# Gather and segment-sum of a graph layer on one core: one-hots in one operation, place and column loaded, slots released by marker products

## The reference

```python
h = jnp.maximum(_layernorm(x, axis=-1), 0.0)
xs = h[src]
for i in range(4):
    msgs = msgs + jnp.where((edge_types == i)[:, None], xs @ W[i] + b[i], 0.0)
return x + jax.ops.segment_sum(msgs, dst, num_segments=12500)
```

## Time and profile before

| | us |
|---|---|
| median of 3 runs | 2328.6 |
| lowest, highest | 2311.18, 2332.2 |
| profiled execution, its own time | 2344.42 |
| its span | 2342.7 |

### The profile page before, as it was taken

The page is one execution under the profiler, slowest core; times in us unless marked ns, Lnnn a source line. Parts: engine busy times, 40 slices in busy tenths (PEclk is TensorE's granted clock), DMA queues, the critical chain, the costliest instruction groups (busy, mean ns, idle before and its releaser), DMA issues.

```text
span 2342.7 us, 19295 instructions
## 1 busy us (share of the span) xinstructions
PE 873.5 (37%) x3921; PEld 641.9 (27%) x3922; DVE 705.6 (30%) x1734; ACT 134.7 (6%) x384; POOL 1484.2 (63%) x1573
## 2 busy tenths in 40 slices
PE   6774133233433343334343433343334233421233
PEld 2232122223322323222222232223222232321123
DVE  5554123233232323232323232323232233221123
ACT  3331000000000000000000000000000000000000
POOL 6666665756665666666666666666666666666763
PEclk8886566666665666666666665666666576665666
DMA  8663111111111111111111111111111111111231
GB/s 247 213 202 106 45 45 40 48 36 46 47 45 40 46 47 44 43 45 47 45 46 45 47 45 42 45 47 45 42 45 47 44 43 45 47 45 45 66 107 53
DMA packets 95454, 144.73 MB, mean 62 GB/s; under 512 B 27481, under 2 KB 57683, under 8 KB 95363
## 3 DMA queue, kind: packets, MB, share of 16 engines
q0 software_dynamic: 50016, 102.50, 16.8%
q1 hardware_dynamic: 40567, 38.92, 5.0%
q10 hardware_dynamic: 4780, 2.51, 0.4%
HBM read 111.73 MB, written 32.09 MB: 61 GB/s over the span
## 4 chain that ended last, share of the span: by engine, by line
another core or an unknown queue 29%; issue 25%; DVEq 24%; PE 10%; DVE 10%; ACT 1%; ACTq 0%; DMA 0%
DVEq L662 4%; PE ps_y L778 4%; DVEq L668 4%; DVEq L643 2%; DVE lists L643 2%; DVE acc L633 2%; PE ps_sum L828 2%; DVEq L633 2%; DVEq L625 2%; PE ps_y L857 2%; DVEq L655 2%; DVEq L663 2%; DVEq L672 2%; DVEq L271 2%
## 5 line engine op out<-in xcount | busy, mean ns | idle before, releaser
L369 POOL DMA_INDIRECT messages<-message_table,table_row x1155 | 1095.9, 949 | 613.3 <-issue 340.0
L828 PE MATMUL ps_sum<-messages,lists 128*128 128x128 f32 x1776 | 272.7, 320 | 570.3 <-DVE acc L633 341.5
L828 PEld LDWEIGHTS ps_sum<-messages,lists 128*128 128x128 f32 x1776 | 259.2, 233 | 581.8 <-issue 581.5
L369 POOL DMA_INDIRECT lists<-message_table,table_row x288 | 272.7, 947 | 147.2 <-issue 83.0
L672 DVE SCALAR_TENSOR_TENSOR ps_node<-node_iota,scaled_iota 128x128 f32<-128x128 f32 x200 | 72.3, 361 | 837.6 <-issue 825.9
L643 DVE SCALAR_TENSOR_TENSOR lists<-ps_node,node_iota,dst_col 128x512 f32<-128x512 f32 x296 | 212.6, 748 | 166.9 <-issue 131.0
L828 PE MATMUL ps_sum<-messages,onehot 128*128 128x128 f32 x582 | 116.8, 383 | 298.3 <-DVE acc L633 173.2
L828 PE MATMUL ps_sum<-lists 128*128 128x128 f32 x592 | 111.3, 366 | 222.8 <-issue 151.1
L828 PEld LDWEIGHTS ps_sum<-messages,onehot 128*128 128x128 f32 x582 | 110.8, 292 | 303.2 <-issue 303.2
L633 DVE SCALAR_TENSOR_TENSOR acc<-ps_sum,own_tile,acc x203 | 70.3, 346 | 357.1 <-remote 161.2
L828 PEld LDWEIGHTS ps_sum<-lists 128*128 128x128 f32 x592 | 106.4, 278 | 226.6 <-issue 226.6
(11 more groups left out here) (87 smaller groups left out, 524.5 us busy)
## 6 DMA issues: line engine op xcount, KB each, us to landing
message_table<-stage SPq DMA_DIRECT2D x98, 256.0 KB
messages<-message_table,table_row POOLq DMA_INDIRECT x1155
out<-acc SPq DMA_DIRECT2D x24, 256.0 KB
lists<-message_table,table_row POOLq DMA_INDIRECT x288
acc<-in_x SPq DMA_DIRECT2D x4, 896.0 KB
early_x<-in_x,src_col POOLq DMA_INDIRECT x119
acc<-in_x ACTq DMA_DIRECT2D x2, 896.0 KB, 6.0
acc<-in_x SPq DMA_DIRECT2D x1, 832.0 KB
```

The costliest lines, as they stand in the source:

```text
L369: pool.indirect_dma_start(messages[k][0:rows, t, :], None, table_rows, bass.IndirectOffsetOnAxis(ap=flat_rows[0:rows, at + t:at + t + 1], ...
L828: ins = nc.tensor.matmul(ps_sum[:, bass.ds(q % BANKS, 1), 0:d], onehots[k][:, t, :], messages[k][:, t, :], start=(t == 0), stop=(t == tile ...
```

## The change

Five edits, all of them in how the engines hand things to each other:

1. VectorE makes the one-hots of a pair in one operation of 8 tiles where it made two of 4 tiles. The semaphores `onehot_ready[0]`, `onehot_ready[1]` and `first_half_done` become one `onehot_ready`, and TensorE waits once ahead of its 8 products.
2. The free first number of `ranges` now holds the column (tile x 128) at which the sum is added. VectorE loads column, place, tile and windows in one go and passes column and place down through registers for three pairs, where it packed both into one number and split it again.
3. TensorE raises `slot_free[k]` by a marker product right behind the products of k, for every superblock but the last. L815 and L816 are gone.
4. ScalarE copies an early superblock's 8 tiles from `early_x` into `stage` once that is free, raises `e_rows_ready`, and applies the relu in place. VectorE's statistics read the copy at fixed addresses and wait for it.
5. The first wait value of a superblock's one-hots is (pair + 1) / 2 instead of 1.

```diff
@@ scalar, early superblocks
+                act.wait_ge(e_used, i + 1)
+                nc.scalar.copy(e_h[:, :, :].rearrange("p t f -> p (t f)"),
+                               flat_early[:, bass.ds(i * (SB_TILES * d), SB_TILES * d)]).then_inc(e_rows_ready, 1)
...
-                act.wait_ge(e_used, i + 1)
                 for t in range(SB_TILES):
-                    nc.scalar.activation(e_h[:, t, :], flat_early[:, bass.ds((i * SB_TILES + t) * d, d)], ACT.Relu,
+                    nc.scalar.activation(e_h[:, t, :], e_h[:, t, :], ACT.Relu,
@@ vector
             def make_onehot(s, home, tiles, tile, needed):
-                for half, (a, z) in enumerate(halves(tiles)):
-                    dve.wait_ge(pair_done if half else first_half_done, needed)
-                    nc.vector.scalar_tensor_tensor(
-                        out=home[:, a:z, :],
...
+                dve.wait_ge(pair_done, needed)
+                nc.vector.scalar_tensor_tensor(
+                    out=home[:, 0:tiles, :],
...
             def next_pair(q):
                 dve.wait_ge(pair_done, q)
-                place_and_tile(low_regs[LAG - 1], add_place_reg, add_tile_reg)
-                add_sums(add_place_reg, add_tile_reg, bass.ds((q + 1) % BANKS, 1), pair_added)
+                add_sums(place_regs[LAG - 1], at_regs[LAG - 1], bass.ds((q + 1) % BANKS, 1), pair_added)
...
-                dve.reg_load([place_reg, tile_reg, windows_reg], flat_ranges[0:1, bass.ds(s * 4 + 1, 3)])
+                dve.reg_load([at_reg, place_reg, tile_reg, windows_reg], flat_ranges[0:1, bass.ds(s * 4, 4)])
...
             def early_rows(i):
+                dve.wait_ge(e_rows_ready, i + 1)
                 for t in range(SB_TILES):
-                    nc.vector.bn_stats(e_stats[:, t, :], flat_early[:, bass.ds((i * SB_TILES + t) * d, d)]).then_inc(e_stats_taken, 1)
+                    nc.vector.bn_stats(e_stats[:, t, :], e_h[:, t, :]).then_inc(e_stats_taken, 1)
@@ tensor
-            def superblock(s, k, tiles, needed, frees, at_once=False):
+            def superblock(s, k, tiles, needed, release_slot=True):
...
-                    for half, (a, z) in enumerate(halves(tiles)):
-                        pe.wait_ge(onehot_ready[half], q)
-                        for t in range(a, z):
...
-                        ins.then_inc(pair_done if half else first_half_done, 1)
+                    pe.wait_ge(onehot_ready, q)
+                    for t in range(tiles):
...
+                    ins.then_inc(pair_done, 1)
                     pe.reg_add(pair_reg, pair_reg, 1)
-                if frees is not None:
-                    pairs_done_since(slot_free[frees])
-                if at_once:
+                if release_slot:
                     nc.tensor.matmul(ps_mark, release[:, 0:1], release[:, 0:1], start=True, stop=True).then_inc(slot_free[k], 1)
```

More of the change, by code:

```diff
@@ L235, in gnn_program @@
     h_sums_ready = sem("h_sums_ready")
-    onehot_ready = [sem(f"onehot_ready{half}") for half in range(2)]
-    first_half_done = sem("first_half_done")
+    onehot_ready = sem("onehot_ready")
     pair_done = sem("pair_done")
@@ L702, in finish_windows @@
                 last = pair()
-                places = [dve.alloc_register(f"dve_last_place_{n}") for n in range(LAG)]
-                ats = [dve.alloc_register(f"dve_last_at_{n}") for n in range(LAG)]
-                for n in range(LAG):
-                    place_and_tile(low_regs[LAG - 1 - n], places[n], ats[n])
                 for n in range(LAG):
@@ L806, in _ @@
             pe.wait_ge(y_ready, node_tiles + 2)
-            pe.sem_inc(first_half_done, LAG)
             pe.sem_inc(pair_done, LAG)
@@ L844, in early_superblock @@
                     pe.wait_ge(e_mask_ready, i + 1)
[L845 to L851 removed]
+                    pe.wait_ge(onehot_ready, q)
+                    for t in range(SB_TILES):
+                        nc.tensor.matmul(ps_y[:, 1, 0:P], type_mask[:, t, :], early_onehot[:, t, :],
+                                         start=(t == 0), stop=(t == SB_TILES - 1))
                     pe.wait_ge(e_h_ready, (i + 1) * SB_TILES)
```

78 lines of the change are left out of this document (33 added, 45 removed).

## The result

The change took 2288.6 us (median of 4 runs, 2277.8 to 2290.5), the kernel before beside it 2326.2 us (4 runs, 2311.2 to 2332.2): ratio 0.984, 95% interval 0.9805 to 0.9875. It is faster by 1.6%, 38 us. The forecast was 78 us: right in direction, twice too large.

The account below looks back on a forecast made before the run. A cycle of late TensorE signals, three superblocks then 4.6 us of GpSimd silence, was taken as the limit. Markers saved 82 us, all else nothing: 2328.6 - 82 = 2247, taken as 2250 us; 8-in-10 range 2200 to 2345.

Parts of the forecast that it names:

- Step (3): Slot release by marker products: four superblocks per cycle in place of three, 66 waits become 49.5, 82 us saved.
- TensorE's stop at L816 is what lets only three through: At TensorE's own wait: it stopped there after the third superblock; without it, TensorE could take a fourth in the slow phase.
- The forecast's own range: For the whole time: 2205 to 2290 us, from 3.5 to 4.5 superblocks per cycle, less 18 us for the copy.
- Step (1): VectorE's one-hots in one operation: counted as nothing beside GpSimd's gathers; without that cover, -40 to +100 us.
- (2): Place and column as loaded: VectorE's instructions per superblock fall from 23 to 19; by itself worth nothing.
- Step (4): ScalarE's copy of early rows: 1.2 us against 5.0 us of cover, counted as nothing; without cover 18 us.
- Step (5): Setup and statistics: one more 0.2 us operation, 8 fixed addresses in place of 8 register ones; nothing.
- The rule on fetches: VectorE's early loop, then in two blocks of 256 instructions at most, would stop refetching; no part in the sum.
- the rival of 2284 us: VectorE's early loop: no fourth superblock, but refetches end, 45 us at most; 2284 us, chance 0.12.
- Locked: GpSimd's cycle: a marker's signal is as late as any, so nothing moves; 2328 us, chance 0.20.
- Slower, by longer silences: GpSimd's slot waits: 9.3 us each where release comes behind TensorE's next product; +44 us, 2373 us, chance 0.14.
- Vanished: GpSimd's slot waits: three slots of slack suffice, up to 328 us go; 2001 to 2150 us, chance 0.04.

Follow-up runs that it names:

- the kernel with half of the products: The changed kernel with 4 of each superblock's 8 products left out: on slow queues 2339.0 us, ratio 1.0081 to the kernel before; on fast queues 0.9989.
- edit (1) alone: The kernel before with only a pair's one-hots in one operation, one TensorE wait and signal per pair: 2306.8 against 2341.4 us, ratio 0.9863, slow queues.
- The kernel with markers alone: The kernel before with only the slot release by marker products: slow queues, five executions of 2355 to 2363 us and one of 2310.2, against 2338.3 us.

## Why the prediction failed, step by step

**Step (3) failed**, and with it the size. It priced a wait at a constant 4.97 us and let the number fall by a fourth superblock per cycle. The number stayed (68 and 68), and without the markers the gain is there too. The price was wrong too: a wait is 1.2 us and 0.14 per gather. Had the fourth superblock come, 16.5 waits fewer would have been worth 16.5 x 1.2 = 20 us, not 82, since the remaining 1443 x 0.14 = 202 us are owed for the gathers whatever their grouping. This stood in the earlier trace rows: 2.25 us is the silence after 8 gathers, 4.6 the one after 24. I took the first for an exception instead of a second point of the line.

**"TensorE's stop at L816 is what lets only three through"** was the reason behind it. Without that stop TensorE works on but doesn't get ahead: one superblock's products took from 2055.7 to 2075.3 us after the change, as long as two superblocks of gathers. The prediction priced the slow phase only for VectorE's queue and gave TensorE's products their fast duration. Its reading of that queue was right in size, though the earlier trace rows pairs two different instructions of L662: at 2056.31 us the load of `ranges`, at 2061.02 the address ahead of it. Like for like the 0.08 us stand against this row, the address in the slow phase (kernel before):

```profile
2054.92 0.69 DVEq L662
```

The load itself took 0.70 us in the slow phase and, by the trace, 0.74 us in the fast one. The two rows of 2054.92 and 2056.31 us also lie 1.4 us apart, not 0.70, so the 16 us that the prediction gave VectorE for a superblock in the slow phase were too few; the rows of the kernel with half of the products have 18 to 20.

The forecast's own range doesn't follow from its terms: 3.5 to 4.5 superblocks per cycle at 4.97 us a wait are 47 to 109 us, 2219 to 2282 us, and up to 2300 with the 18 us of (4), not 2205 to 2290.

**Step (1), counted at nothing, holds the gain.** The range for it was -40 to +100 us with the cover gone, and measured alone it is 35 us faster. The steady cycle does cover it, as said; the cover is missing behind early superblocks, where TensorE and VectorE have the work of two superblocks to do before GpSimd may go on, and six of fifteen times weren't done when the queues recovered. The waits' sum over what the line gives, 68 x 1.2 + 202 = 284 us, was 48 us before and is 3 us after; the six waits alone, 60.0 us where the line has 18.4, are 42 us of it. That this excess is the early superblocks' work is read from where the waits lie and from edit (1)'s removing five of the six. Why edit (1) gets that work done in time is argued, not shown. (2), also counted at nothing, adds nothing measurable.

**Step (4)** at nothing was right: without the copy 2301.7 us on a chip where edit (1) alone took 2306.8. **Step (5)** was right in that nothing shows.

**The rule on fetches.** By the packets, two blocks for VectorE and a refetch at a taken branch describe the queue well: 84 became 23, and a shift by jumped-over code made 25 of the unchanged loop, as the Trainium skill (Runtime: NRT & Kernel Launch, section Instruction fetch mechanics) would have it. The stall that the same section of the Trainium skill warns of has no price that shows here: ratio 1.0017 (0.9987 to 1.0046) with the packets gone. Giving fetches no part in the sum was right, and the rival of 2284 us, nearest in number to 2288.6, came near it by luck: what it priced, the length of the early rounds, is where the gain lies, but fetches aren't what made them long.

**The other rivals.** Locked was right about the cycle and wrong about the time, since it forgot the rounds with early superblocks. Slower, by longer silences: no wait of 9 us in the changed kernel came from the release itself. The kernel with markers alone was slower in five of six executions, with waits of 7.3 to 10.2 us at early superblocks; that these are the longer silence of this rival isn't shown. Vanished: didn't come on slow queues, and with fast queues no traced kernel has a wait for a slot.

## What to carry to other kernels

Before pricing a stall as number times mean, sort its instances by what preceded each: a stall that grows with the work since the last one is a rate, and regrouping it saves only the constant part. Look for the rounds that are longer than the steady ones, and take work off what is in them: that was nearly the whole gain here, 42 of the 44.5 us of waits. And a change worth 1.3 to 1.6% in some comparisons cost 0.2% in another, so a kernel bounded by GpSimd's gathers should be timed on more than one chip and at more than one time.

## What the runs showed of the hardware

The kernel before takes 1975.5 to 1976 us in the comparisons with fast queues and 2321 to 2341 us in the rest, 18% more, with the same gather of 0.944 to 0.952 us. The first stage differs too: the first gather of messages starts at 157 to 160 us with fast queues and at 189 to 195 us in the rest. With slow queues, while GpSimd issues gathers, a register instruction on VectorE's queue takes 0.70 us where it takes 0.08 after a silence, and a record of TensorE's products comes every 1.4 to 2.8 us in the changed kernel, while the register instructions of TensorE's queue keep their 0.03 to 0.3 us (2050 to 2076 us). Each gather, at a step of 1.25 us, leaves 0.14 us that is worked off only when none is issued. What this consists of no run shows, but that it isn't the gathers' own packets. The Trainium skill (GPSIMD Engine Reference, section 4. When to use GPSIMD) says that GpSimd's own cores generate the descriptors of such transfers and ring the doorbells; no run here shows whether these have a part in it, nor why the same chip has slow queues at one time only.
